# Narrow attention layers: products of probabilities with values issued two sets at a time

## The reference

```python
attn = jnp.einsum('bhqd,bhkd->bhqk', q, k) / np.sqrt(HD)
attn = jax.nn.softmax(attn, axis=-1)
out = jnp.einsum('bhqk,bhkd->bhqd', attn, v)
out = out.transpose(0, 2, 1, 3).reshape(B, L, D)
return out @ Wo + bo
```

## Time and profile before

| | |
|---|---|
| median of three runs | 6146.87 us |
| span of the profiled execution | 6151.9 us |
| TensorE matmul busy | 5766.3 us, 94% |
| TensorE weight load busy | 3017.5 us, 49% |
| VectorE busy | 4377.2 us, 71% |
| ScalarE busy | 4138.0 us, 67% |
| GpSimd busy | 2794.9 us, 45% |
| mean granted TensorE clock | 0.977 |

### The profile page before, as it was taken

The page is one execution under the profiler, slowest core; times in us unless marked ns, Lnnn a source line. Parts: engine busy times, 40 slices in busy tenths (PEclk is TensorE's granted clock), DMA queues, the critical chain, the costliest instruction groups (busy, mean ns, idle before and its releaser), DMA issues. The chain is left out here.

```text
span 6151.9 us, 76991 instructions
## 1 busy us (share of the span) xinstructions
PE 5766.3 (94%) x28528; PEld 3017.5 (49%) x28528; DVE 4377.2 (71%) x4761; ACT 4138.0 (67%) x6776; POOL 2794.9 (45%) x2156
## 2 busy tenths in 40 slices
PE   8999999999999998899998899999999999999998
PEld 5545445555545554454544444444444444444444
DVE  5666654434444435567665898989898998989897
ACT  3444545544455543444436889989898999989896
POOL 0000002222222221001001887969696987969696
PEclk8999999999999999999999999999999999999999
DMA  4313122000000003232232202020201102020200
GB/s 127 56 32 62 32 52 25 2 2 2 3 1 2 2 2 55 41 60 45 45 66 46 33 21 61 28 55 30 51 30 43 40 21 60 30 53 30 51 30 19
DMA packets 168727, 222.47 MB, mean 36 GB/s; under 512 B 37154, under 2 KB 104059, under 8 KB 168099
## 3 DMA queue, kind: packets, MB, share of 16 engines
q1 hardware_dynamic: 168354, 217.55, 16.4%
HBM read 152.90 MB, written 30.49 MB: 30 GB/s over the span
## 5 line engine op out<-in xcount | busy, mean ns | idle before, releaser
L2387 DVE TENSOR_TENSOR_SCAN l__h<-l__decay,psum 128x1024 f32<-128x1024 f32 x1024 | 2246.3, 2263 | 54.3 <-POOL l__hc L2365 20.5
L2365 POOL TENSOR_TENSOR l__hc<-l__h,l__c_rep 128x1024 f32<-128x1024 f32 x1016 | 2013.7, 2012 | 131.0 <-DVE l__h L2387 76.2
L1959 ACT ACTIVATE l__decay<-l__dt_rep,l__a_neg 128x511 f32<-128x511 f32 x2048 | 1340.5, 709 | 31.4 <-DVE l__h L2387 31.1
L1969 PEld LDWEIGHTS psum<-ident,l__dtx_B 128*128 128x128 f32 x8192 | 887.3, 142 | 901.1 <-DVE l__h L2387 603.2
L2490 PE MATMUL psum<-l__hc,l__gather 128*64 128x512 f32 x4096 | 1113.8, 622 | 139.1 <-POOL l__hc L2365 137.3
L1969 PE MATMUL psum<-ident,l__dtx_B 128*128 128x128 f32 x8192 | 1124.3, 281 | 68.2 <-DVE l__h L2387 39.9
L1943 ACT ACTIVATE l__dtx_B<-l__dtx_T,l__b_T 128x512 f32<-128x512 f32 x1664 | 1103.3, 709 | 2.5 <-PEq L1289 1.3
L693 DVE TENSOR_REDUCE l__row_max<-psum 128x1 f32<-128x512 f32 x1024 | 655.5, 686 | 232.5 <-PE psum L708 231.6
L1418 POOL TENSOR_SCALAR l__probs<-l__probs,l__rec 128x512 f32<-128x512 f32 x512 | 350.1, 697 | 914.2 <-DVE l__rec L1414 914.1
L197 POOL TENSOR_SCALAR l__ln_var_eps<-l__ln_mean_var 128x4 f32<-128x4 f32 x57 | 16.4, 288 | 1635.4 <-DVE l__ln_mean_var L183 1635.4
L1040 ACT ACTIVATE l__probs<-psum 128x1024 f32<-128x1024 f32 x512 | 501.9, 1023 | 273.1 <-PE psum L1112 268.9
(11 more groups left out here) (173 smaller groups left out, 6590.6 us busy)
## 6 DMA issues: line engine op xcount, KB each, us to landing
l__c_rep<-l__c_dram SPq DMA_DIRECT2D x512, 128.0 KB, 2.8
l__dt_rep<-l__dt SPq DMA_DIRECT2D x128, 256.0 KB, 5.1
l__parts_dram<-l__parts SPq DMA_DIRECT2D x64, 384.0 KB, 3.5
l__q_stack<-l__parts_dram SPq DMA_DIRECT2D x192, 128.0 KB, 6.3
l__k_stack<-l__parts_dram SPq DMA_DIRECT2D x192, 128.0 KB, 9.0
l__w<-in_l_w SPq DMA_DIRECT2D x6, 1024.0 KB, 7.6
l__gate_rows<-l__gates_dram SPq DMA_DIRECT2D x24, 256.0 KB, 3.3
in_mod_w<-in_mod_w SPq DMA_DIRECT2D x1, 4608.0 KB, 17.2
```

Source lines behind the costliest of these rows:

```text
L1959: nc.scalar.activation(decay[:, i % DECAYS, s, 1:T], dt_rep[:, w, c, s, 1:T], ACT.Exp, scale=a_neg[:, g, c, s:s + 1]).then_inc(S["decay"], 1)
L1969: last = nc.tensor.transpose(bx_psum(i)[:, s, t * P:(t + 1) * P], dtx_B[:, (k + 1) % 2, t, 2 * c + s, :, :].rearrange("p j d -> p (j d)"), ...
L2365: nc.gpsimd.tensor_tensor(hc[:, i % HCS, :, :], h[:, i % HS, :, :], c_of(i), ALU.mult).then_inc(S["hc"], 1)
L2387: nc.vector.tensor_tensor_scan(both(h[:, i % HS, :, :]), both(decay[:, i % DECAYS, :, :]), both(bx_psum(i)), 0.0, ALU.mult, ALU.add).then_ ...
```

## The change

The sets are issued two at a time, on m % 8 == 3 instead of m % 4 == 3, starting at m = 11. V0 and V1 come behind S36, V2 and V3 behind S44, V4 and V5 behind S52, V6 and V7 behind S60, V8 and V9 at m = 43, V10 and V11 at m = 51, V12 and V13 at m = 59, V14 and V15 at m = 67. The second set of every two keeps its place, and the first moves back by four tiles to stand ahead of it. What a set computes and its waits are unchanged, and so are the programs of the other engines.

```diff
--- before.py
+++ after.py
@@ -1175,8 +1175,9 @@
                     if F and n == SPREADS_AT[0]:
                         pe.wait_ge(*F.S.at("hT", DC))
                     spread(SPREADS_AT.index(n))
-                if m > GH and m % GH == 3 and m < TILES + GH:
-                    values(m // GH - 1)
+                if m > 2 * GH and m % (2 * GH) == 3 and m < TILES + GH:
+                    for q in (m // GH - 2, m // GH - 1):
+                        values(q)
 
             pe.wait_ge(*S.at("exp", TILES // 2))
             pe.wait_ge(*S.at("oT_norm", NG - 1))
```

## The result

The changed kernel takes 6159.57 us (median of 13 runs) against 6146.69 us for the kernel before (13 runs). The ratio is 1.0024, with a 95% interval from 1.0016 to 1.0032: slower by some 15 us, 10 to 20, going by the ratio; the two medians differ by 12.9 us. The forecast was slower, 6168 us, in a range from 6148 to 6184.

A forecast was written before the change was run, and what follows sets the result against it. TensorE was taken as the bound, VectorE only 7% behind, with ScalarE limiting after the last score tile. The parts sum to +1.30 us per batch, times 16 +21 us, giving 6168 us, range 6148 to 6184.

The forecast's parts named there:

- The saving per joint: Joining two sets saves TensorE 0.24 us; seven new joints per batch make 1.68 us, 27 us over 16 batches.
- (a): S32 to S37, the first sets: new waits of 0.97 us against 0.24 saved, with the earlier wait gone; +0.21 us.
- (b): Eight tiles without rows of maxima, S37 to S45 and S53 to S61: 5.86 us instead of 5.67, +0.19 each.
- (c): Eight tiles with rows of maxima, S45 to S53: the double set lies over VectorE's 1.32 us; -0.15 us.
- The recurrence of the three-bank ring: Score tiles wait for VectorE: a maximum every 0.61 us, started 0.43 behind its matmul, TensorE continuing 0.05 after VectorE ends.
- the price of a ring wait: TensorE's cost per wait, taken as 0.05 us; at nothing or 0.10, the sum moves 0.3 us per batch.
- (d): S61 to the row sums: exponentials set the pace, waits rise from 0.75 to 1.84 us, two joints save 0.48; +0.61.
- (e): Row sums to V14: V12 no longer covers the reciprocals; +0.49 us at full clock, +0.20 at 1.2 GHz, taken as +0.25.
- the same ring: Each layer's last batch has extra next-layer work in the loop, but was counted like the others, +1.30 us.
- The first rival: Gaps are saved and VectorE's idle time absorbs the bursts: -1.68 us per batch, 6120 us; chance 0.13.
- gains and waits cancel: Second rival: shorter ring waits, or less low clock in part of the batches; about 6147 to 6155 us, chance 0.2.
- more low clock: Third rival: longer 1.2 GHz from the row sums to V14 in every batch, +25 us on top, 6193 us; chance 0.1.

The follow-up runs named there:

- short maxima: Row maximum over 256 of 512 columns: on the kernel before, ratio 0.9955; with sets 0 to 7 also joined in twos, 0.9936.
- three pairs of banks: Transposed tiles use three pairs of banks, not two, from tile 48 on: kernel before 6134.3 us, changed kernel 6157.48 us, one run each.
- V12 alone: The changed kernel, but V12 stands by itself behind the row sums again, all other joints kept; ratio 1.0020 to the kernel before.
- V12V13 alone: The kernel before with only V12 and V13 joined, all other sets as they were; ratio 1.0013 to the kernel before.

## Why the prediction was right, and where it was off

**The saving per joint**, 0.24 us: the double set takes 1.85 us as in the earlier trace rows. With short maxima a joint gives 0.18 us in each part (b), where a wait of 0.06 us for the ring is left, and more in the two parts that have rows of maxima, 0.44 in (a) and 0.48 in (c), 1.28 us in all. That each change of the tiling mode drains TensorE, as the Trainium skill says ("TensorEngine Tiling (Array Packing)", Key Properties), agrees with the trace: the saving is there where nothing waits. That it is the tiling, and nothing else in a set, that makes the gap, no run here shows.

**(a)** forecast +0.21, measured +0.14 in the median and +0.02 in the mean, as the three shorter batches were not foreseen. **(b)** +0.19 twice, measured +0.18 twice, 5.85 us against my 5.86. **(c)** -0.15, measured -0.17, 6.45 against 6.47. The recurrence of the three-bank ring, from 0.61, 0.43 and 0.05 us, held to 0.02 us in (b) and (c), so the price of a ring wait, the unknown that I had bounded, made no difference there.

**(d)** forecast +0.61, measured +0.43. The prediction counted waits by starts, and so counted they come to 0.41 us at P40, 0.04 at the transposes, 0.93 at P48 and 0.39 at P50, 1.77 us against the 1.84 forecast. Before, they come to 0.51 at P48, 0.23 at P54 and 0.14 at the row sums, 0.88 us against my 0.75: I had left out the row sums' wait. Both errors went the same way. I also wrote that the DMA of the rows "is then hidden". It is not: it ends P48's wait together with the exponential, and with three pairs of banks 0.73 us of wait for it remain. Split by runs, V8V9 gains 0.29 us and V10V11 costs 0.72, of which the third pair of banks gives back 0.45.

**(e)** forecast +0.25, measured a median of +0.67 and a mean of +0.39. The failing step is that at 1.2 GHz the pairs "cover nearly the whole wait". That is so only where the low clock begins right behind the row sums, as in four of the thirteen batches (9.5 to 9.7 us, no loss). In seven (10.28 to 10.35 us) it began later, the wait of 0.83 us by starts stood bare at 2.4 GHz, and the double set was slowed instead of the pairs. The low clock then cost about as much as before, and the joint cost what it costs at the full clock. For that I had +0.49 us; in the changed kernel with three pairs of banks the one batch without low clock takes 8.67 us, against 7.99 with V12 alone, +0.68. In the last two the low clock lasted 6.8 us.

The parts sum to +1.15 us, or +1.03 by the mean of (a), where I had 1.30. **The last batch of each layer** was the other gap: I wrote "the same ring". They lose 2.6 and 3.3 us, and in both a double set right behind longer waits runs at 1.2 GHz: V2 and V3 in layer 0 (the third stretch above), V10 and V11 in layer 2. That makes S37 to S45 8.81 us in the one and S61 to the sums 15.01 in the other, where the other of the two last batches, at the full clock in that part, has 7.14 and 13.36. Even these are 0.86 and 1.08 us more than before. The next layer's work stands on VectorE among the maxima (L191) and on ScalarE among the exponentials (L146), so a bank of the ring and a pair come free later. VectorE in layer 0, ScalarE in layer 2, then TensorE's timeline in layer 2:

```profile
846.16 1.37 DVE L191 TENSOR_SCALAR l__ln_xn<-x_sb,l__ln_mean_var,l__ln_rstd 128x256 f32<-128x256 f32 x4
...
3267.40 1.44 ACT L146 ACTIVATE l__hT<-psum,l__cur_ahead 128x512 f32<-128x512 f32 x2
```

```profile
3269.81 0.96 PE L1112 MATMUL psum<-l__q_stack,l__k_stack 99*128 99x512 bf16 x2 [1.57 <-ACT l__probs L1040]
3270.70 3.20 PE L1125 MATMUL psum<-l__probs,l__v_and_ones 128*32 128x512 f32 x16
```

That the waits brought the low clock was not tried apart.

**The total**: 19.7 us in the two layers of the profiled execution, 21 forecast, and 15 (10 to 20) by the ratio of the runs. That 19.7 and 21 lie so close is in part luck: the ordinary batches lost 1.03 us where 1.30 was forecast, and the last ones about 3 where 1.30 was.

The first rival (gains without waits) is right in (c) and with short maxima, wrong elsewhere: VectorE's 0.30 us of idle time per four tiles was indeed not enough. The second (gains and waits cancel, up to 6155 us) lies below the measured 6159.57. The third (more low clock) came true in the last batches, in two of the thirteen others, and in most batches of the kernel with V12V13 alone.

## What to carry to other kernels

Work that no other engine waits for is cover: joining it saves its gaps only if the queues on both sides are deep enough for the burst, here three banks at 0.61 us against 1.85 us of silence did not do, and three banks with a maximum over half the columns did. Place such work where the issuing engine waits anyway; the same sets joined over one wait gave 10 us, and moved forward into it 23 to 32 us, of which 8 to 14 stand behind the row sums, where only the clock differs, while joining them evenly lost 15. Read it per batch from distances between starts, when unchanged layers move by 10 us between executions.

## What the runs showed of the hardware

The stretch at 1.2 GHz behind the 24 narrow matmuls of the row sums has no fixed place: in the batches shown it began between 0.9 us before their end and 1.7 us after it, lasted 3.4 or 6.8 us, and in several batches of other kernels was absent. With V12 alone behind the row sums it makes this part 7.99, 9.6 or 11.2 us long with identical instructions. Over 16 batches that can be as much as the change itself, and a change's effect on it can't be read from the moved instructions alone.
